# A Gated DeltaNet and FFN block on one core: a new order of the steps on all five engines

## The reference

```python
qkvz = (hidden_states @ w_qkvz.T)          # 32 heads of q, k, v, z, 64 wide each
mixed = causal depthwise convolution over 4 taps of q, k, v
g = -exp(A_log) * softplus(a + dt_bias);  beta = sigmoid(b)
q = l2norm(q) * DK ** -0.5;  k = l2norm(k)
# for every token t, a 64 x 64 state for each sequence and head:
Sstate = Sstate * exp(g_t)
kv     = k_t @ Sstate
delta  = (v_t - kv) * b_t
Sstate = Sstate + outer(k_t, delta)
o_t    = q_t @ Sstate
o = o * rsqrt(mean(o * o) + EPS) * norm_weight * sigmoid(z);   out = o @ w_out.T
# FFN: fwht is a Walsh-Hadamard transform
y = silu(fwht(x * SU_ug) @ W_gate.T * scale) * (fwht(x * SU_ug) @ W_up.T * scale)
out += fwht(y * SU_dp) @ W_down.T * scale
```

## Time and profile before

| what | value |
|---|---|
| median of 3 runs | 844.16 us (843.19 to 848.38) |
| profiled execution, its own time | 839.25 us |
| its span, first to last instruction | 837.5 us |
| PE busy | 743.5 us, 89% of the span |
| DVE busy | 688.2 us, 82% |
| ACT busy, POOL busy | 326.3 us, 39%; 278.0 us, 33% |
| mean granted TensorE clock | 0.974 |

### The profile page before, as it was taken

The page is one execution under the profiler, slowest core; times in us unless marked ns, Lnnn a source line. Parts: engine busy times, 40 slices in busy tenths (PEclk is TensorE's granted clock), DMA queues, the critical chain, the costliest instruction groups (busy, mean ns, idle before and its releaser), DMA issues.

```text
span 837.5 us, 27042 instructions
## 1 busy us (share of the span) xinstructions
PE 743.5 (89%) x11562; PEld 490.0 (59%) x11562; DVE 688.2 (82%) x1224; ACT 326.3 (39%) x737; POOL 278.0 (33%) x186
## 2 busy tenths in 40 slices
...
DMA packets 131703, 49.28 MB, mean 59 GB/s; under 512 B 111488, under 2 KB 121088, under 8 KB 131456
## 3 DMA queue, kind: packets, MB, share of 16 engines
...
## 4 chain that ended last, share of the span: by engine, by line
PE 48%; DVE 15%; SPq 14%; DMA 10%; issue 7%; ACT 4%; POOL 2%; DVEq 0%; ACTq 0%; POOLq 0%
PE bank L715 15%; SPq L641 4%; PE bank L863 4%; PE bank L835 4%; SPq L665 4%; DVE kq L259 3%; DMA UU<-base_blocks 3%; PE bank L743 3%; PE bank L736 3%; SPq L667 3%; PE bank L806 3%; PE bank L915 2%; DMA inverse_blocks<-UU 2%; DMA base_blocks<-ATP 2%; PE bank L848 2%
## 5 line engine op out<-in xcount | busy, mean ns | idle before, releaser
L715 PE MATMUL bank<-xnT,wq 128*128 128x512 f32 x512 | 254.4, 622 | 1.3 <-DVE kq L259 1.1
L259 DVE SCALAR_TENSOR_TENSOR kq<-bank,cw,kq 128x510 f32<-128x510 f32 (+2 forms) x288 | 213.6, 745 | 17.9 <-ACT kq L1043 11.0
L715 PEld LDWEIGHTS bank<-xnT,wq 128*128 128x128 f32 x512 | 90.8, 194 | 83.4 <-issue 72.1
L1043 ACT ACTIVATE kq<-bank,cw 128x512 f32<-128x512 f32 x96 | 65.8, 687 | 174.8 <-PE bank L715 146.6
L1231 POOL TENSOR_TENSOR Sd<-St,dec 128x256 f32<-128x256 f32 x32 | 22.6, 706 | 276.5 <-DVE St L383 224.0
L1235 POOL TENSOR_TENSOR ost<-ost,cst 128x8 f32<-128x8 f32 x32 | 53.8, 1680 | 134.1 <-DVE ost L396 134.0
L1225 POOL TENSOR_TENSOR kqg<-kq,rows 128x1024 f32<-128x1024 f32 x32 | 77.4, 2438 | 41.9 <-DVE kq L259 41.9
L915 PE MATMUL bank<-wo,oT 128*128 128x256 f32 x256 | 68.2, 384 | 0.0
L1195 POOL TENSOR_TENSOR stat<-stat,cst 128x16 f32<-128x16 f32 x16 | 46.3, 2896 | 39.8 <-DVE nV L318 39.8
L736 PE MATMUL bank<-xh,wguT 128*128 128x512 f32 x128 | 57.9, 595 | 0.0
L371 DVE TENSOR_TENSOR X<-U,bank 128x256 f32<-128x256 f32 (+1 forms) x96 | 42.8, 460 | 17.9 <-PE bank L804 8.2
...
## 6 DMA issues: line engine op xcount, KB each, us to landing
...
base_blocks<-ATP SPq DMA_DIRECT2D x128, 16.0 KB, 1.8
...
```

The source lines that it names most:

```text
L259: nc.vector.scalar_tensor_tensor(out=y[:, :, t:S], in0=p[:, :, 0:S - t], scalar=cw[:, m, i // 2, 3 - t:4 - t], in1=y[:, :, t:S], op0=ALU.m ...
L715: last = nc.tensor.matmul(ring[i % 2][:], wq[:, q, kc, i // 2, :], xnT[:, kc, (i % 2) * 512:(i % 2) * 512 + 512], start=kc == 0, stop=kc = ...
L1043: nc.scalar.activation(kq[:, i // 2, 2 * (i % 2):2 * (i % 2) + 2, :], split(ring[i % 2][:], 2), ACT.Copy, scale=cw[:, m, i // 2, 3:4]).the ...
```

## The change

The five strings of step names are replaced by five others. Every string holds the same names as before, each once, so that the instructions are the same; only their order on each engine changes, from pair 0 to pair 15. On PE the stretch of pair 15 alone keeps its order. Of the strings the diff shows one line of SP's, cut:

```diff
-0.rload 1.rload 0.bout 0.bin 2.load 2.fload 2.rload 0.uout 0.uin 1.oload 1.bout 3.load 1.bin 1.uout 1.uin 3.rload 2.oload
+0.rload 1.rload 0.bout 1.oload 0.bin 2.load 2.fload 2.rload 0.uout 0.uin 1.bout 1.bin 2.oload 3.load 1.uout 1.uin
```

More of the change, by code:

```diff
@@ L539, in _ @@
[L539 to L540 removed]
+                         "state": state, "norm": norm, "gated": gated, "turn": turn, "out": out, "fold": fold, "fo": fo}, """0.fold 0.proj.0 0.proj.1 0.proj.2 0.proj.3 0.e 0.proj.4 0.stats 0.proj.5 0.gram.0 0.gram.1 0.ff 1.e 0.gram.2 0.gram.3
@@ L543, in _ @@
[L543 to L546, removed]
@@ new lines, in _ @@
+                     1.ks.2 2.inv.2 1.state.2 1.norm.0 1.ks.3 3.stats 1.gated.0 3.proj.5 1.norm.1 1.turn.0 3.gram.0 3.gram.1 1.gated.1
+                     1.out.0 1.turn.1 1.out.1 3.gram.2 2.vtr.0 1.out.2 1.out.3 3.gram.3 2.vtr.1 4.proj.0 4.proj.1 2.hz.1.0 2.hz.1.1
+                     2.hz.2.0 2.hz.2.1 2.hz.3.0 2.hz.3.1 4.e 2.state.0 3.inv.0 2.ks.1 3.inv.1 4.proj.2 2.state.1 4.proj.3 2.ks.2 2.norm.0
+                     4.proj.4 2.state.2 2.gated.0 2.ks.3 3.inv.2 2.turn.0 2.norm.1 4.proj.5 2.gated.1 2.out.0 2.turn.1 4.stats 2.out.1
@@ new lines, in _ @@
+                     4.hz.3.1 6.proj.0 6.proj.1 4.state.0 5.inv.0 4.ks.1 5.inv.1 4.state.1 6.proj.2 4.ks.2 4.norm.0 6.proj.3 4.state.2
+                     6.proj.4 4.ks.3 4.gated.0 5.inv.2 4.turn.0 4.norm.1 6.proj.5 4.gated.1 4.out.0 4.turn.1 6.stats 4.out.1 6.gram.0
+                     4.out.2 6.gram.1 5.vtr.0 4.out.3 5.vtr.1 6.ff 6.gram.2 6.gram.3 5.hz.1.0 5.hz.1.1 5.hz.2.0 5.hz.2.1 7.e 5.hz.3.0
+                     5.hz.3.1 7.proj.0 7.proj.1 5.state.0 6.inv.0 5.ks.1 6.inv.1 5.state.1 7.proj.2 5.ks.2 5.norm.0 7.proj.3 5.gated.0
@@ new lines, in _ @@
+                     5.state.2 7.proj.4 5.ks.3 6.inv.2 5.turn.0 5.norm.1 7.proj.5 5.gated.1 5.out.0 5.turn.1 7.stats 7.gram.0 6.vtr.0
+                     5.out.1 5.out.2 7.gram.1 5.out.3 6.vtr.1 7.ff 7.gram.2 7.gram.3 6.hz.1.0 6.hz.1.1 6.hz.2.0 6.hz.2.1 8.e 6.hz.3.0
+                     6.hz.3.1 8.proj.0 8.proj.1 6.state.0 7.inv.0 6.ks.1 7.inv.1 6.state.1 8.proj.2 6.ks.2 6.norm.0 8.proj.3 6.state.2
+                     8.proj.4 6.ks.3 6.gated.0 7.inv.2 6.turn.0 6.norm.1 8.proj.5 6.out.0 6.gated.1 6.turn.1 8.stats 7.vtr.0 7.vtr.1
@@ new lines, in _ @@
+                     6.out.1 6.out.2 8.gram.0 6.out.3 8.gram.1 8.ff 8.gram.2 8.gram.3 7.hz.1.0 7.hz.1.1 7.hz.2.0 7.hz.2.1 9.e 7.hz.3.0
+                     7.hz.3.1 9.proj.0 9.proj.1 7.state.0 8.inv.0 7.ks.1 8.inv.1 7.state.1 9.proj.2 7.ks.2 7.norm.0 9.proj.3 7.state.2
+                     7.gated.0 7.ks.3 9.proj.4 8.inv.2 7.turn.0 7.norm.1 9.proj.5 7.gated.1 7.out.0 7.turn.1 7.out.1 9.stats 7.out.2
+                     8.vtr.0 9.gram.0 7.out.3 9.gram.1 9.ff 8.vtr.1 9.gram.2 9.gram.3 8.hz.1.0 8.hz.1.1 8.hz.2.0 8.hz.2.1 10.e 8.hz.3.0
```

285 lines of the change are left out of this document (137 added, 148 removed).

## The result

The new order takes 815.22 us (median of 4 runs, 812.92 to 817.84), the order before 845.19 us (4 runs, 843.19 to 848.38). The ratio is 0.964 with a 95% interval of 0.960 to 0.969: faster by 3.6%, some 30 us, where 13.7 us were forecast. Ratios, here and in the table further down, leave out executions that took over 1.5% more than the fastest of their kernel, while medians are of all, so that a ratio is not the quotient of two medians (the before runs beside e9 to e12 have a median of 845.5 us, those of them that count 840.1). In the profiled executions the gain is 26.3 us (839.25 to 812.92 us); before's one was a quick execution of that order.

A forecast was written before the change was run, and what follows sets the result against it. PE (743.5 of 837.5 us busy) was taken as the bound, so only its idle time and clock could be won: 16.9 + 1.9 - 5.1 = 13.7 us off the 844.2 us median gives 830.5 us, range 821 to 842.

The forecast's parts named there:

- the cause at the largest: Pair 0: DVE's 1.inv.0 waits for UU, returned late behind 3.load, holding hz steps PE needs; 6.0 us gain booked.
- what was to be seen: Signs: UU wait under 6 us, pair 0 gap under 2, pair 4's hz 9 to 13 earlier, 11.delta.0 12 to 16.
- Against it: new waits: Loss from waits the new order creates across the stretches: 5.1 us, bounds 1 and 14.
- priced by number: Unseen new waits: some fourteen reordered stretches, a 1 us stall in three or four, 3.3 us lost.
- the booked places: Eight places, ahead of pair 0 and in pairs 0, 1, 2, 4, 5, 11, 13, to win 16.9 us together.
- pair 1 1.0: inv.0 behind hz.2 ends a 2.35 us wait, but DVE is late next; 1.0 us gain, bounds 0 and 2.05.
- pair 4 1.4: PE's 1.38 us issue stop in hz.1 amid SP's load traffic goes as 7.load moves; 1.4 us, bounds 0 and 2.8.
- clock in the other places: Low clock after waits outside pair 0: up to 1.26 us per projection, half taken for three places, 1.9 us gain.
- Half given back: Rival: DVE becomes the bound and returns half of the 13.7 us; 837 us; chance 0.18.
- Collisions: Rival: DVE steps meet GpSimd's kqg more often, three more meetings cost 7.2 us; 838 us; chance 0.11.
- Slower by GpSimd: Rival: root and kd steps delay GpSimd's sd and norm, holding DVE and PE; 848 us if all uncovered; chance 0.06.
- the change does nothing: Rival: DMA waits move along with the order; 844 us, within 3; chance 0.08.

The follow-up runs named there:

- e9: The new order with one thing put back on DVE: 12.inv.0 and 12.inv.1 again ahead of 11.hz.2.1; 819.6 us.
- e12: The order before up to the stretch of pair 6, the new order behind it, on all engines; 837.2 us.
- e1: The order before with 3.load, 4.rload, 8.load and 12.fload moved behind the bin of pairs 1, 3, 6 and 13 on SP; 841.0 us.
- e2: e1 plus later places on DVE for seven inv steps of pairs 1, 2, 3, 11, 12 and 14; 841.7 us.
- e16: The new order with 5.kqg.0 behind 3.norm.1 and 10.kqg.0 behind 8.norm.1 on GpSimd, as before; 817.9 us.
- e18: The new order unchanged, run again on another chip as a base; 815.1 us.
- e6: e2 with 4.rload ahead of 3.bout and 4.fload behind 2.uout on SP; 838.4 us.
- e10: e6 with 7.load moved behind 5.bin on SP, as in the new order; 836.3 us.
- e3: The new order with SP alone in its old order; 845.9 us.
- e8: The order before with only DVE and GpSimd in their new order; 882.9 us.

## Why the prediction was wrong, step by step

**Right:** what bounds the kernel, most of the places, and the cause at the largest. The wait for UU is gone, bin of pair 1 returns in 2.1 us, PE has no gap in the hz of pair 0, and the window from 120 to 140 us has clock 1.00; e1 and e2 show the two parts of that place one by one (3.6 us for the load, 2.4 for inv.0). Of what was to be seen, the second half of hz.1 of pair 4 comes 18.9 us earlier, not 9 to 13 (287.07 against 305.94), and 11.delta.0 28 us, not 12 to 16 (614.68 against 642.73).

**The first step that failed: "Against it: new waits", 5.1 us.** The stretches without a booked gain won 1.3 us net, with -2.8 us in pairs 6, 8 and 9 and +4.1 in 3, 7, 10, 14 and 15: 6.4 us of the error. The 3.3 us "priced by number" stood on no row. The 1.8 us were for two kqg ahead of 3.norm.1 and 8.norm.1, and DVE does not wait for ost there: its four waits of 1.0 to 1.2 us are in pairs 10, 11, 12 and 14, in the new order and with the two kqg put back (e16, 4.7 us, as in e18).

**The second step that failed: the sizes of the booked places.** Booked, and measured between the two profiles: pair 0 6.0, 7.1; ahead of it 1.5, 2.1; pair 1 1.0, 3.2; pair 2 2.3, 3.3; pair 4 1.4, 3.6; pair 5 1.7, 2.7; pair 11 1.5, 1.1 (with 12); pair 13 1.5, 2.0. Together 16.9 and 25.1 us; all but those of pairs 11 and 13 lie over their upper bounds. The bounds were taken from one wait of PE for each place. PE's idle time in the stretches named fell by 17.5 us, where 14.1 were booked; in pair 4 it fell by 2.8 us, since there were two stops (1.38 and 2.11 us) and one of 0.68 is left, in pair 1 by 2.1. PE's busy time in them fell by 5.5 us, where 1.3 was booked for pair 0 and 1.9 for "clock in the other places". A wait brought a stretch at 1.2 GHz behind it that lasted longer than one projection, for which the earlier trace rows had shown 3.17 us against 1.91. From pair 0 to the end the clock is worth some 5.3 us (PE busy 657.7 and 652.4 us) against 3.2 booked: the clock is the smaller part of the error. In pair 1 the mechanism was wrong too: PE's stop of 2.05 us did not hang on UU (e1, e2, e6, e10), and DVE was not late next.

**The rest, 2.6 us,** is that the gain was taken from an execution of before that was 4.9 us under its median; the forecast said so but carried the difference over unchanged. So 15.3 us of error (830.5 less 815.2) are 6.3 (8.2 on the places less the 1.9 booked as clock), 6.4 (new waits) and 2.6.

**The rivals.** Half given back: no, the gain came whole, with DVE at 84% of the span (82% before). Collisions: no, the 32 first products of inv.1 took 9.8 us, against 12.3. Slower by GpSimd: a trace of it, 3.4 us more wait for ost, hardly any on PE. That the change does nothing was wrong for the change and nearly right for e1 and e2, where one edit of mine made another load late.

**What stays open.** How much of before's 30 us the late return and the early inv.0 were. Taken out of before, and with 4.rload early, they give 6.8 us (e6); pair 0 alone holds 6.7 in the trace; put back they cost 27.6, partly at places where before lost nothing. A rival was not excluded: that any old piece in the new order costs this much because it does not fit, as e3 and e8 do for other pieces. Why the later inv.0 gains in pairs 11 to 14 only in the new order (e2, e6: nothing or a loss) was not settled. The order on PE and ScalarE differs there too; the new string of PE or of ScalarE alone was not tried.
